# Seven loops of a graph network kernel written out as straight code

## The reference, cut to what matters

```python
# product pass: messages per edge, multiplied over the edges of a node
bf = jnp.exp(coeff * (dist[:, None] - centers[None, :]) ** 2)
bf = ssp(bf @ W1 + b1)
bf = ssp(bf @ W2 + b2)
msg = h[src] * edge_feat * bf * cut[:, None]
agg = jax.ops.segment_prod(msg, dst, num_segments=n_nodes)
out = ssp(agg @ W3 + b3)

# attention, three times
h = x @ W
al_s = h @ a_src
alpha = leaky_relu(al_s[s] + al_d[d] + al_e, 0.2)
ex = jnp.exp(alpha - segment_max(alpha, d)[d])
out = segment_sum(h[s] * (ex / denom[d])[:, None], d) + bias
```

## Time and profile before

| what | value |
|---|---|
| three runs | 9977.71, 9978.89, 9986.97 us |
| the profiled execution, its own time | 9988.77 us |
| its span | 9985.9 us |
| mean granted clock of TensorE | 0.676 |
| instructions recorded | 101845 |
| busy: PE, DVE, POOL, ACT | 53%, 51%, 49%, 20% of the span |

### The profile page before, as it was taken

How to read it: one execution, slowest core, us unless ns; L and a number is a source line. 1 busy time by engine, 2 the same in 40 slices (tenths; PEclk the granted TensorE clock), 3 DMA queues, 4 the chain that set the end, 5 groups by cost and what they waited for, 6 DMA issues and landing times. The chain is left out here.

```text
span 9985.9 us, 101845 instructions
## 1 busy us (share of the span) xinstructions
PE 5278.3 (53%) x25982; PEld 3376.7 (34%) x25982; DVE 5128.3 (51%) x17152; ACT 2006.9 (20%) x3703; POOL 4889.7 (49%) x5045
## 2 busy tenths in 40 slices
PE   4555555555367676999940555331265423055532
PEld 3333322332234444444420334321135422033432
DVE  6665556666568887000010787430297623077744
ACT  5555633333236555000000000000000001000000
POOL 5666555565456664000047126657506665713664
PEclk7767666666677777999975556665556656555656
DMA  5444455555235555888843013112203212302311
GB/s 164 133 131 138 133 146 165 166 168 166 62 114 190 188 185 188 302 289 283 291 128 98 15 59 100 50 49 76 62 15 101 71 35 61 101 12 60 102 49 32
DMA packets 728900, 1216.85 MB, mean 122 GB/s; under 512 B 109340, under 2 KB 547085, under 8 KB 714832
## 3 DMA queue, kind: packets, MB, share of 16 engines
q1 hardware_dynamic: 552716, 847.76, 25.5%
q0 software_dynamic: 161120, 311.32, 12.3%
q10 hardware_dynamic: 14688, 53.48, 1.4%
HBM read 865.31 MB, written 346.85 MB: 121 GB/s over the span
## 5 line engine op out<-in xcount | busy, mean ns | idle before, releaser
L1008 POOL DMA_INDIRECT RO<-table,src_t x2346 | 2256.3, 962 | 3346.4 <-DMA table<-H 1244.0
L978 POOL DMA_INDIRECT RO<-table,src_t x2346 | 2290.9, 976 | 1532.8 <-issue 673.5
L1969 DVE TENSOR_TENSOR acc<-acc,PS 128x128 f32 x3910 | 1110.5, 284 | 1532.3 <-remote 1067.7
L1573 PE MATMUL PS<-RO 128*128 128x128 f32 x3060 | 670.3, 407 | 1189.4 <-DMA RO<-table,src_t 716.0
L2392 DVE SCALAR_TENSOR_TENSOR H<-iota_row,srchi_t,PS 128x49 f32<-128x49 f32 x2352 | 496.9, 386 | 1082.6 <-remote 652.3
L1573 PEld LDWEIGHTS PS<-RO 128*128 128x128 f32 x3060 | 621.8, 310 | 1236.2 <-DMA RO<-table,src_t 737.1
L1646 PE MATMUL PS<-als_bf,RO 128*128 128x49 bf16 x7056 | 397.7, 218 | 1193.3 <-issue 891.8
L2198 DVE TENSOR_SCALAR RO<-PS,loc_t,shared 128x128 f32<-128x128 f32 x2346 | 957.2, 410 | 0.6
L1646 PEld LDWEIGHTS PS<-als_bf,RO 128*128 128x128 bf16 x7056 | 327.7, 118 | 1483.1 <-issue 1112.1
L1488 PEld LDWEIGHTS PS<-RO 128*128 128x128 f32 x3128 | 580.6, 279 | 224.2 <-issue 110.9
L1488 PE MATMUL PS<-RO 128*128 128x128 f32 x3128 | 589.3, 365 | 123.0 <-DMA RO<-table,src_t 57.5
(11 more groups left out here) (403 smaller groups left out, 8416.4 us busy)
## 6 DMA issues: line engine op xcount, KB each, us to landing
GT<-adjacency SPq DMA_DIRECT2D x126, 1792.0 KB, 7.2
adjacency<-H SPq DMA_DIRECT2D x98, 1568.0 KB
RO<-adjacency SPq DMA_DIRECT2D x42, 1792.0 KB, 7.2
RO<-table,src_t POOLq DMA_INDIRECT x4692
staged<-RO ACTq DMA_DIRECT2D x102, 512.0 KB
H<-staged SPq DMA_DIRECT2D x102, 512.0 KB
soft_rows<-shared SPq DMA_DIRECT2D x196, 256.0 KB
H<-soft_rows SPq DMA_DIRECT2D x98, 512.0 KB
```

The lines of the kernel that those rows point to most:

```text
L978: pool.indirect_dma_start(rows[:, h * HT + j, :], None, table[k % 2], at(src_t[:, t:t + 1]))\
L1008: pool.indirect_dma_start(rows[:, g % 2 * HT + j, :], None, table[k % 2], at(src_t[:, t:t + 1]))\
L1573: last = mm(PS[:, o:o + D], block[:, j * D:(j + 1) * D], onehot[:, h * HT + j, :], start=True, stop=True)
L1969: tt(at, at, window_at(k, c, j), ALU.add).then_inc(added[h], 1 if j < n - 1 else HT - n + 1)
```

## The change

The seven `Fori` loops (two on SP, one on ACT, two on PE, two on DVE) become Python loops, so every iteration is written out with constants for semaphore values and addresses. All eleven calls of `hold` and its definition go. Nothing else changes: the same operations, in the same order on each engine. The core of the diff:

```diff
-        def hold(eng):
-
-            eng.nop(nofuse=True)
-
@@ SP: soft rows, cut-off rows
                 wait(sp, z_ready[1], i * 2 + h - 1)
-                hold(sp)
                 sp.dma_start(half(soft, h), soft_rows[:, ds(i * BE + h * HE, HE)]).then_inc(soft_in[h], 16)
...
                     wait(sp, keep_bc, i * 2 + h - 1)
-                    hold(sp)
@@ SP: low digits in attention, the product pass
-                    with sp.Fori(0, ITERS) as i:
+                    for i in range(0, ITERS):
...
-                    with sp.Fori(2, ITERS - 1) as i:
+                    for i in range(2, ITERS - 1):
@@ ACT: product slots (hold goes before the first activation and the copy)
-                    hold(s)
...
-                    with s.Fori(1, ITERS - 2) as i:
+                    for i in range(1, ITERS - 2):
@@ PE: attention, product slots
-                with pe.Fori(0, ITERS - 1) as i:
+                for i in range(0, ITERS - 1):
...
-                    with pe.Fori(1, ITERS - 2) as i:
+                    for i in range(1, ITERS - 2):
@@ DVE: product slots (hold goes in five of their operations)
                     wait(v, msg_turned, i * 2 + h - 1)
-                    hold(v)
...
-                with v.Fori(1, ITERS - 2) as i:
+                for i in range(1, ITERS - 2):
@@ DVE: attention (hold goes in make_lo and pick)
                     v.wait_ge(al_rows[h], i + l * ITERS)
-                    hold(v)
...
-                with v.Fori(0, ITERS - 1) as i:
+                for i in range(0, ITERS - 1):
```

## The result

The changed kernel takes 10025.67 us, the median of 8 runs (9999.39 to 10044.65); the kernel before, run beside it, 9989.06 us (8 runs, 9977.71 to 9995.44). The ratio is 1.0036, 95% interval 1.0025 to 1.0047: slower by a third of a per cent. "No change" was forecast. The time lies inside the range, but 46.8 us above the median of the three runs that the forecast started from, beyond the 20 us that it took for "no change".

What follows compares the result with a forecast made beforehand. Bounds: PE's increments queued behind POOL's gathers (product pass, slow attention), DVE's own instructions (fast attention). Terms 0 + 0 - 3 + 0 + 0 + 0 = -3 us, from the median 9978.89 to 9976 us; range 9925 to 10040.

Steps and rivals of the forecast that it cites:

- No change: Whole kernel: 9976 us against a median of 9978.89, within the 20 us a measurement cannot tell; chance 0.58.
- Parts 1, 2 and 5: Loop branches, register arithmetic of attention's picks, and attention's slow part: each taken as 0, hidden or off the path.
- The price of a branch in part 1: DVE's attention loop: compare-and-branch 0.056 us, three loop instructions 21.2 us over 144 passes, hidden under a 1.40 us comparison.
- Part 6: Fetching the longer written-out code, some 85 more PE packets of 16 KB: taken as 0.
- rival B: Slower: code fetching stalls PE and DVE in attention's fast part, 10032 to 10258 us; chance 0.19.
- the rule of the Trainium skill: Straight code streams with block crossings mostly hidden, a taken branch breaks the prefetch; by it 0 to -20 us.
- part 4: SP's queue in the product loop: transfers issued earlier by at most a few us, nobody on the chain waits; 0.
- part 3: Empty instructions removed: product pass chain loses 0.07 us x 46 = 3 us at L2246; bounds 0 and 7 us.
- the pause of POOL at 5.8 us: Sign to check in the product pass: pause unchanged, iteration near 25.5 us; below 5 us would mean rival A.
- Rival A: Faster: PE's increments get through earlier in the product pass, up to 147 us, or 49 us for a third; chance 0.23.
- The reading of the earlier trace: Layer 0's edge pass, straight code, also shows a PE matmul every 1.4 us, so written-out code does not end the queue.

Runs made afterwards that it cites:

- attention_straight: Only the three attention loops (SP, PE, DVE) written out, product pass as in the kernel before; ratio to the kernel before 0.9991 (0.9982 to 1.0000).
- product_straight: Only the product pass's four loops written out, without their empty instructions, attention as in the kernel before; ratio to it 1.0044, repeated on another chip 1.0031.

## Why the prediction was wrong

**The steps that held.** Parts 1, 2 and 5, branches, arithmetic of the picks and the slow part of attention, at 0: the fast part is 241.3 us from first to last comparison against 241.1, the slow parts have seven halves as before, and attention_straight measured 0.9991 with its upper bound at 1.0000. The price of a branch in part 1 was too low, which cost nothing under its cover: a compare-and-branch of DVE's attention loop is 0.056 us long, but where it is taken the sequencer's next instruction starts 0.29 us after it (0.10 us where the loop ends). Part 6 and rival B, fetching code: 226 packets came against some 233 foreseen, and the fast part's groups show nothing of them (5600.3 to 5841 us):

```profile
L2377 DVE SCALAR_TENSOR_TENSOR H<-iota_row,srchi_t,PS 128x49 f32<-128x49 f32 x718 | 140.1, 261 | 0.0
L2366 DVE TENSOR_SCALAR RO<-PS,iota_col 128x1024 bf16<-128x1024 f32 x90 | 115.2, 1280 | 0.0
L1638 PE MATMUL PS<-als_bf,RO 128*128 128x49 bf16 x2153 | 106.0, 218 | 49.6 <-DVE RO L2366 49.6
```

DVE is idle for 0.0 us before both, and PE waits for DVE alone: 19.2 matmuls and loads of PE per microsecond of straight code at no cost (0.4 us of idle time in the earlier trace rows). The means of 261 and 1280 ns, for 385 and 1402 in the earlier trace rows, are no gain: a half takes 2.68 us in both traces, and product_straight, whose attention loops are those of before, records 255 and 1274 ns as well. By the rule of the Trainium skill that the prediction had quoted (Runtime: NRT & Kernel Launch, section Instruction fetch mechanics) the crossing of a block is mostly hidden, and the trace agrees. For the stall at a branch the same section sets a condition that the prediction left out, a target outside the two pages held. A pass of PE's attention loop is 104 matmuls and loads, an estimated half of a packet at the prediction's 223 a packet. So 0.9991 (0.9982 to 1.0000) neither confirms nor refutes that rule.

**The step that failed** is the sum over a chain taken as fixed, in part 4 and the last figure of part 3. Part 4 took 0 for SP's earlier transfers with the words "Nobody on the chain waits for them", and part 3 took 3 us off a chain that it took as given: gathers, PE's increment, L2246, L2229. SP's part alone did measure nothing (0.9996), and so did that of the other three engines (0.9995); both together gave 1.0044. What the sum lacked is a term for the pause itself. That chain is only one of the places at which a late increment can be caught. The prediction's own check, "the pause of POOL at 5.8 us", named the thing that broke: 17 of the 37 pauses are over 9 us, and these wait ahead of L2242, not of L2235, which was L2246. Rival A had the right material, a queue in which PE's increments stand while POOL gathers, but only a gain was drawn from it. The rival on the slow side was set on fetching, which shows no cost here; that the time lies inside the range, whose upper part stood for it, is luck. The missing rival reads: a small shift of the engines changes which increments fall behind the gathers, and the price of the other rhythm is 1.1 us per half, some 100 us over the pass if it held throughout, 46 us as it came.

The reading of the earlier trace rows, that the delay is not a matter of loops, was right, and stronger than it was used. In the product pass it needs no transfers of SP either.

**What stays open.** Why increments are late on some chips; that was never in the kernel's hand. What tips the rhythm: only SP's part with that of the other three engines did, SP with one other engine was not tried where increments are late, and no run with all four engines straight spaced SP's transfers as the loop does. How much of the loss is the rhythm: on a chip without late increments, where there is none, the changed kernel itself was not run, and with one empty instruction before each of SP's transfers it measured 1.0016 (1.0007 to 1.0025), 13 us; four variants with the product pass straight measured 1.0007 to 1.0011 there, only one interval (1.0002 to 1.0020) clear of 1, and no profile of the kernel before was taken. No version beats the kernel before beyond doubt; the one with only the attention loops straight comes closest, at 0.9991.

## What to carry to other kernels

Where a profile shows a wait for an increment that was due long ago, don't take the pause as a constant: find what is caught in it, and what would be caught if an engine were a little earlier. Here a steady rhythm was a state that a neutral edit left, so forecast both directions, with the price of the next rhythm as a rival. Look in the trace, too, whether a delay that an experiment puts in is really there. And compare chips before tuning around such a wait: on two of the five here it did not exist.

## What was not expected of the hardware

- On some chips, semaphore increments of PE arrive late while POOL issues indirect gathers one after the other, and in the long pauses are released some 3 to 4 us after the last one ends, with SP's transfers or without (the two pauses shown above). On others such code shows 0.01 us. This is worth 18% of this kernel: 9945 to 10013 us against 8127 to 8129, of which the attention layers make 1160 us (661.7, 636.8 and 639.1 us from first to last comparison, against 258.8 to 259.6 in variants of the kernel) and the product pass some 220.
- With late increments PE issues one instruction per 1.4 us in the slow part of attention, and the granted clock doesn't tell the two kinds of chip apart there: it is 0.50 (1.2 GHz) in that layer on both.
- Twelve empty instructions in a row on SP left one in the trace and no more time between transfers than one did (0.48 us from the stored products to the cut-off rows in both).
- Transfers beside the gathers do cost where increments are prompt: the pass took 977.9 us without SP's transfers and 1010 to 1019 us with them.
